# Normalizing the last five tiles of a transform one by one instead of together

## The chip, the cores and the metric

The kernel runs on one core of a Trainium2 chip. The metric is the device time of one execution in microseconds. Engines are called as in the profile: PE is TensorE (PEld its weight loads), DVE is VectorE, ACT is ScalarE, POOL is GpSimd, SP is SyncE.

## The reference, cut to what matters

A graph network of four layers on 1250 nodes with 512 features. The change lies at the end of the first layer, whose second part computes, for 21250 edges,

```python
hb = einsum('nd,bdo->bno', h, basis1)              # four bases
m = (sum over b of comp1[etypes][:, b] * hb[b][src]) * norm
out = segment_sum(m, dst) + bias1 + h @ loop1
x = layernorm(x + out)                             # mean and variance over 512 columns, eps 1e-5
```

The next layer then gathers rows of this `x` by `src`, again for 21250 edges.

## The kernel before, in words

The nodes lie in ten tiles of 128 rows (NT = 10, HALF = 5). A part of a layer has two stages. `aggregate` gathers rows with indirect DMAs that POOL issues (`gather`, L740), multiplies them on PE by a selector (L788), adds them into `G` on DVE (L909) and turns the sums with PE transposes. `transform` then multiplies the turned sums by the bases.

`transform` runs over 32 steps in the part that matters here: two halves of five tiles, and in each half four bases by four blocks of 128 rows. In a step ACT rounds the left side and the weights (L1267, L1269), DVE and POOL make the remainders (L1285, L1297), and PE does three matmuls for each of the five tiles (L136 to L138, in `split_matmul`), tile j into PSUM bank j. Only the fifteenth matmul of a step counts up the semaphore `product` (`multiplied`). Where there is no bias, as here, the epilogue takes "the half is summed" from that semaphore.

The epilogue is `ResidualNorm`. For the first half its work is strewn between the steps of the second (`between_on_dve`, `between_on_act`). For the second half it comes behind the last step, as five instructions of each kind in a row:

- DVE, in `add` (L1202), adds bank j to the residual tile in SBUF, five times, after it has waited for the whole half; then it waits until these are done.
- DVE, in `moments`, does five `bn_stats` (L1004), waits, five `bn_aggr` (L1007), and in `add_eps` one addition of eps to the five variances (L1019).
- ACT, in `root` (L1024), takes the five square roots in one instruction.
- DVE, in `norm`, takes five reciprocals in one instruction (L1029), and subtracts and multiplies each tile in place (L1032, a `tensor_scalar` with the mean and the reciprocal as scalars of a partition), five times.
- ACT, in `store`, waits for each tile and issues its store to `x1_rows` (L1177, 256 KB each, on ACT's own DMA queue).

What comes next in program order is `aggregate` of the second layer. Its first instruction on POOL is a memset of 24 windows of the new `G` (L747, 128 by 12288 fp32 in SBUF), which waits only until the last left side of the transform has been read. Everything else, on PE, ACT, DVE and POOL alike, waits for the list `ready`: the last product, the ten normalized tiles and the landing of all five stores:

```python
ready = multiplied + [residual.ln.normed.now()] + [s.now() for s in residual.stored]
```

POOL then issues the gathers, at first eleven, and each later one when the matmul that frees its buffer is done. DVE builds the selectors (L843, L850), and ACT zeroes the other 57 windows of `G` (L823). The third transform (second layer) has a bias, and its own epilogue lies partly in the third layer.

Of the kernel before, what the change touches and what calls it, by code (L numbers as in the profile page):

```python
# [5 lines left out]
ALU = mybir.AluOpType  # L6
ACT = mybir.ActivationFunctionType
# [16 lines left out]
HALF = NT // 2  # L24
# [105 lines left out]
def tile_rows(r, j):  # L130
    return r[j * P:(j + 1) * P, :]


def split_matmul(pe, acc, lhs, rhs, start, stop):

    pe.matmul(acc, lhs[0], rhs[0], start=start, stop=False)  # L136
    pe.matmul(acc, lhs[0], rhs[1], start=False, stop=False)  # L137
    return pe.matmul(acc, lhs[1], rhs[0], start=False, stop=stop)  # L138


def prepare(C):
# [292 lines left out]
    def on_pe():  # L434
# [4 lines left out]
        for n in range(at_product[PATHC, "windows", 0], len(products)):  # L439
            multiply(n)  # L440

    on_dve()
    on_pe()
    pool.wait_ge(*taken(at_product[PATH0, "src", 0] + 1))
# [10 lines left out]
def sort_edges(C, load_edges):  # L455
# [66 lines left out]
    on_sp()  # L522
    on_pool()
    on_dve()
    cleared = C.event("sort_cleared")
    for engine in (act, pool):
# [13 lines left out]
class Coefficients:  # L540
# [133 lines left out]
    def on_dve(self):  # L674
        for k in range(len(self.batches)):
            self.compare(k)
            if k and self.complete(k - 1) is not None:
                self.weigh(k - 1)
        self.weigh(len(self.batches) - 1)
# [22 lines left out]
def aggregate(C, path, nb, co, rows, G, slots, ready, free=(), cleared=0, counting=None,  # L702
# [216 lines left out]

    on_pool()  # L920
    on_act()
    on_pe()
    on_dve()
    M.at = space
    if counting:
# [110 lines left out]
class TransposeX:  # L1036
# [26 lines left out]
    def on_act(self):  # L1063
        act = self.C.act
        for j in range(0, NT, 2):
            act.wait_ge(*self.turned(j + 1))
            act.copy(*self.moved(j)).then_inc(*self.by_act.inc())
        act.wait_ge(*self.by_dve(NT // 2))
# [72 lines left out]
class ResidualNorm:  # L1141
# [24 lines left out]
        pass  # L1166

    def on_act(self, half):
        self.ln.root(HALF, half + 1)
        self.store(half)  # L1170

# [24 lines left out]
    def add(self, half):  # L1196
# [5 lines left out]
            dve.tensor_tensor(self.tile(j), C.bank[j % HALF][:], self.tile(j), ALU.add).then_inc(*self.added.inc())  # L1202
        dve.wait_ge(*self.added.now())

    def on_dve(self, half):
        tiles = [self.tile(j) for j in range(half * HALF, (half + 1) * HALF)]
        self.add(half)
        self.ln.moments(tiles)
        self.ln.norm(tiles, half + 1)


def transform(C, products, bias, ready, epilogue, extra=None, beside=0, other=None):

    M, bank = C.M, C.bank
    pe, act, dve, pool, sp = C.engines
    ring = M.new("weight_ring", [P, 4, D])
    weight_parts = M.new("weight_parts", [P, 2, 2, D], F32R)
    lhs_parts = M.new("lhs_parts", [P, 2, 2, HALF, P], F32R)  # L1220
    brow = M.new("bias_row", [1, D])
    steps = [(half, m, k) for half in range(2) for m in range(len(products)) for k in range(KC)]
    middle = len(steps) // 2
    chunk_in = [C.landed(f"chunk{r}_in") for r in range(4)]
    bias_in = C.landed("bias_rows_in")
    lhs_hi, lhs_lo = C.event("lhs_hi"), C.event("lhs_lo")
    weight_hi, weight_lo = C.event("weight_hi"), C.event("weight_lo")
    multiplied, summed = C.event("product"), C.event("half_summed")
    epilogue.summed = summed if bias is not None else lambda half: multiplied(half * middle)
    epilogue.half_read = lhs_lo(middle)  # L1230
    if other:
        other.half_read, other.weight_lo = lhs_lo(middle), weight_lo

    def on_sp():
        for token in ready:
            sp.wait_ge(*token)
        if bias is not None:
            sp.dma_start(brow[:], bias.rearrange("(a d) -> a d", a=1)).then_inc(*bias_in.inc())
        for n, (half, m, k) in enumerate(steps):
            if n == middle + 4:  # L1240
                epilogue.on_sp(0)
            if extra and n == extra.at - 6:
                extra.load()
            if extra and 4 <= n < 4 + NT // 2:
                for j in range(2 * (n - 4), 2 * (n - 4) + 2):
                    C.count_store.row(j)
            if other and n >= middle:
                other.on_sp(n - middle)
            if n >= 4:
                sp.wait_ge(*weight_lo(n - 4 + 1))  # L1250
            sp.dma_start(ring[:, n % 4, :], products[m][1][k * P:(k + 1) * P, :]).then_inc(*chunk_in[n % 4].inc())
        epilogue.on_sp(1)

    def on_act():
        for token in ready:
            act.wait_ge(*token)
        for n, (half, m, k) in enumerate(steps):
            if extra and n == extra.at:
                extra.on_act()
            if n > middle:  # L1260
                epilogue.between_on_act(n - middle)
            if other and n >= middle:
                other.on_act(n - middle)
            lhs = products[m][0](k, range(half * HALF, (half + 1) * HALF))
            if n >= 2:
                act.wait_ge(*multiplied(n - 2 + 1))
            act.copy(lhs_parts[:, n % 2, 0], lhs).then_inc(*lhs_hi.inc())  # L1267
            act.wait_ge(*chunk_in[n % 4](n // 4 + 1))
            act.copy(weight_parts[:, n % 2, 0, :], ring[:, n % 4, :]).then_inc(*weight_hi.inc())  # L1269
        if not other:  # L1270
            epilogue.on_act(1)

    def on_dve():
        for token in ready:
            dve.wait_ge(*token)
        for n, (half, m, k) in enumerate(steps):
            if extra and n == extra.at:
                extra.on_dve()
            if n > middle:
                epilogue.between_on_dve(n - middle)  # L1280
            if other and n >= middle:
                other.on_dve(n - middle)
            lhs = products[m][0](k, range(half * HALF, (half + 1) * HALF))
            dve.wait_ge(*lhs_hi(n + 1))
            dve.tensor_tensor(lhs_parts[:, n % 2, 1], lhs, lhs_parts[:, n % 2, 0].bitcast(F32),  # L1285
                              ALU.subtract).then_inc(*lhs_lo.inc())
        if not other:
            epilogue.on_dve(1)

    def on_pool():  # L1290
        for token in ready:
            pool.wait_ge(*token)
        for n in range(len(steps)):
            if other and n >= middle:
                other.on_pool(n - middle)
            pool.wait_ge(*weight_hi(n + 1))
            pool.tensor_tensor(weight_parts[:, n % 2, 1, :], ring[:, n % 4, :],  # L1297
                               weight_parts[:, n % 2, 0, :].bitcast(F32), ALU.subtract).then_inc(*weight_lo.inc())

    def on_pe():  # L1300
        for token in ready:
            pe.wait_ge(*token)
        for n, (half, m, k) in enumerate(steps):
            if extra and n == extra.at - 1:
                extra.on_pe()
            if other and n >= middle:
                other.on_pe(n - middle)
            s = n % 2
            pe.wait_ge(*lhs_lo(n + 1))
            pe.wait_ge(*weight_lo(n + 1))  # L1310
            for j in range(HALF):
                if n == middle:
                    epilogue.wait_for_bank(j)
                ins = split_matmul(pe, bank[j][:], [lhs_parts[:, s, q, j, :] for q in range(2)],
                                   [weight_parts[:, s, q, :] for q in range(2)], m == 0 and k == 0,
                                   bias is None and n % middle == middle - 1)
            ins.then_inc(*multiplied.inc())
            if n % middle == middle - 1:
                if bias is not None:
                    pe.wait_ge(*bias_in(1))  # L1320
                    for j in range(HALF):
                        ins = pe.matmul(bank[j][:], C.ones[0:1, :], brow[:], start=False, stop=True)
                    ins.then_inc(*summed.inc())
                epilogue.on_pe(half)

    on_sp()
    on_act()
    on_dve()
    on_pool()
    on_pe()  # L1330
    return [multiplied.now(), summed.now()], [lhs_lo(len(steps) - beside)]

# [44 lines left out]
def layers_0_1(C):  # L1377
# [19 lines left out]
    hidden = Hidden(C, h, xT, hidden_rows)  # L1397
    turn_x = TransposeX(C, x, xT, 4 * KC)
    multiplied, free = transform(C, products + [(plain_lhs(xT), A["L0_gnn_loop0"])], A["L0_gnn_bias0"], turned, hidden,
                                 turn_x, KC)  # L1400
    assert M.at <= tail
# [176 lines left out]
def layer_2(C):  # L1578
# [145 lines left out]
    on_sp()  # L1724
    on_pe()
    on_act()
    on_dve()
    C.layer2_done = [z_taken.now(), degree.now(), turned_act.now(), turned_dve.now(), C.conditioned]
# [874 lines left out]
```

## Time and profile before

| | |
|---|---|
| median of 3 runs | 3517.71 us (3515.36 to 3524.45) |
| time of the profiled execution | 3515.15 us |
| its span | 3513.8 us |
| PE, DVE, ACT, POOL busy | 91%, 55%, 40%, 34% of the span |
| mean granted PE clock | 0.974 |

The span is the time between the first and the last instruction that the profiler saw; 1.35 us of the execution's time lies around it. The profile's busy shares are averages over stages with different limits, so one stage has to be read from the timeline and the chain of waits.

### The profile page before, as it was taken

Reading aid. Unit: us, or ns where it says so; the run is one execution under the profiler, and the core shown is the slowest. Engines: PE = TensorE matmul, PEld = TensorE weight load, DVE = VectorE, ACT = ScalarE, POOL = GpSimd, SP = SyncE. Lnnn points to the kernel's source line nnn. Section 1 sums busy time; section 2 is a strip of 40 time slices with the busy share of each in tenths; the row PEclk is TensorE's granted clock in tenths of the full one; section 3 lists DMA queues with packets and bytes.
Section 4 is the critical chain, followed back from the end, with each engine's and each line's share of the span. In section 5 each row is a group of like instructions: output and inputs, shape, how many; then the busy total and the mean of one; then the engine's idle time right before and its main releaser. Section 6 shows DMA issues by size and latency. Waiting matters only on the chain.

```text
span 3513.8 us, 38688 instructions
## 1 busy us (share of the span) xinstructions
PE 3186.8 (91%) x13432; PEld 2126.0 (61%) x13432; DVE 1926.9 (55%) x4296; ACT 1417.8 (40%) x2263; POOL 1186.4 (34%) x1003
## 2 busy tenths in 40 slices
PE   5999898999977788999988999999999999989998
PEld 2333576444742246775456777777777776777767
DVE  6999522887357763245363446544365444754356
ACT  6888632001340023342244553245432554435444
POOL 3666335776367763342000012300132001410022
PEclk8999998999999999999999999999999999999999
DMA  3555433766247763333011001300113001120012
GB/s 85 160 162 161 157 115 103 203 198 183 77 135 211 210 191 103 87 95 114 12 51 42 7 31 44 114 13 7 60 39 95 7 7 61 49 86 7 7 60 72
DMA packets 137266, 318.07 MB, mean 91 GB/s; under 512 B 25380, under 2 KB 43108, under 8 KB 136046
## 3 DMA queue, kind: packets, MB, share of 16 engines
q0 software_dynamic: 53040, 173.84, 17.4%
q1 hardware_dynamic: 82590, 139.10, 12.6%
q8 instruction: 110, 1.80, 0.2%
q10 hardware_dynamic: 1440, 2.62, 0.2%
q14 instruction: 86, 0.70, 0.1%
HBM read 269.50 MB, written 24.84 MB: 84 GB/s over the span
## 4 chain that ended last, share of the span: by engine, by line
PE 71%; DVE 14%; ACT 6%; issue 6%; DVEq 2%; DMA 1%; POOL 1%; SPq 1%; POOLq 0%; ACTq 0%
PE bank L136 11%; PE bank L138 11%; PE bank L137 11%; PE bank L788 10%; PE bank L2282 10%; PE bank L2267 5%; DVE G L909 4%; PE bank L798 3%; PE bank L1983 2%; PE bank L1632 2%; ACT prob L2354 2%; ACT probT L2330 1%; PE bank L766 1%; DVE x_stats L1918 1%; DVE y_tile L1935 1%
## 5 line engine op out<-in xcount | busy, mean ns | idle before, releaser
L788 PE MATMUL bank<-gathered,selector 128*128 128x512 f32 x1326 | 669.1, 619 | 130.6 <-DVE G L909 88.9
L909 DVE TENSOR_TENSOR G<-G,bank 128x512 f32 x663 | 453.7, 684 | 168.6 <-PE bank L788 96.2
L788 PEld LDWEIGHTS bank<-gathered,selector 128*128 128x128 f32 x1326 | 217.2, 194 | 424.4 <-issue 361.2
L2399 DVE CUSTOM_DVE_ANT_0 prob<-bank,count_by_src 128x512 f32<-128x512 f32 (+1 forms) x480 | 258.5, 589 | 316.2 <-PE bank L138 316.2
L2282 PE MATMUL bank<-probT,values_and_heads 128*128 128x512 f32 (+1 forms) x960 | 366.7, 522 | 6.0 <-DVE values_and_heads L2380 6.0
L1297 POOL TENSOR_TENSOR weight_parts<-weight_ring,weight_parts 128x512 fp32r<-128x512 f32 x136 | 199.9, 1471 | 391.5 <-ACT weight_parts L1269 391.5
L2330 ACT COPY probT<-bank 128x512 f32<-128x512 f32 (+1 forms) x480 | 199.0, 488 | 291.7 <-PE bank L2267 291.7
L814 ACT ACTIVATE sign_src<-node_iota_16bit,src_float 128x1280 bf16<-128x1280 f16 x208 | 282.2, 1361 | 50.9 <-PE bank L798 45.0
L775 ACT COPY G<-bank 128x512 f32<-128x512 f32 x160 | 81.3, 659 | 546.2 <-PE bank L766 546.2
L136 PE MATMUL bank<-weight_parts,lhs_parts 128*128 128x512 f32 x680 | 271.7, 400 | 29.4 <-POOL weight_parts L1297 26.6
L1285 DVE TENSOR_TENSOR lhs_parts<-G,lhs_parts 128x640 fp32r<-128x640 f32 x128 | 107.2, 838 | 336.4 <-ACT lhs_parts L1267 336.2
L740 POOL DMA_INDIRECT gathered<-in_x,src_index x208 | 219.2, 1054 | 162.4 <-PE bank L788 100.0
L137 PE MATMUL bank<-weight_parts,lhs_parts 128*128 128x512 f32 x680 | 269.7, 397 | 0.0
L138 PE MATMUL bank<-weight_parts,lhs_parts 128*128 128x512 f32 x680 | 269.0, 396 | 0.0
L740 POOL DMA_INDIRECT gathered<-x_rows,src_index x247 | 233.5, 945 | 92.0 <-issue 50.9
L2111 POOL TENSOR_TENSOR lhs_parts<-values_and_heads,lhs_parts 128x512 fp32r<-128x512 f32 x80 | 107.4, 1347 | 418.0 <-ACT lhs_parts L2091 417.6
L2354 ACT ACTIVATE prob<-prob,negated_max 128x1250 f32<-128x1250 f32 x160 | 218.9, 1368 | 70.3 <-DVE negated_max L2406 70.3
L1836 POOL CAST head_weights_hi<-head_weights 128x1024 fp32r<-128x1024 f32 x16 | 16.6, 1036 | 675.8 <-DMA head_bias_cols<-in_L_gnn_bk 675.8
L2282 PEld LDWEIGHTS bank<-probT,values_and_heads 128*128 128x128 f32 x960 | 172.2, 191 | 114.8 <-issue 108.1
L2267 PE MATMUL bank<-ident,prob 128*128 128x128 f32 x1600 | 204.9, 275 | 30.1 <-ACT prob L2354 29.7
L136 PE MATMUL bank<-kT_hi,qT_hi 128*128 128x512 f32 (+1 forms) x480 | 203.7, 424 | 21.7 <-DVE span_max L2399 17.0
L740 POOL DMA_INDIRECT gathered<-hidden_rows,src_index x208 | 197.5, 950 | 75.9 <-issue 43.6
(272 smaller groups left out, 6225.8 us busy)
## 6 DMA issues: line engine op xcount, KB each, us to landing
weight_ring<-in_L_gnn_basis SPq DMA_DIRECT2D x64, 256.0 KB, 2.7
weight_ring<-in_L_gnn_bases SPq DMA_DIRECT2D x64, 256.0 KB, 2.6
x_L<-x_rows SPq DMA_DIRECT2D x50, 256.0 KB, 4.4
x_rows<-x_L SPq DMA_DIRECT2D x40, 256.0 KB, 2.0
yT_hi<-yT_new_hi SPq DMA_DIRECT2D x4, 2560.0 KB, 10.9
yT_lo<-yT_new_lo SPq DMA_DIRECT2D x4, 2560.0 KB, 10.9
count_rows<-count SPq DMA_DIRECT2D x10, 640.0 KB, 5.6
count_by_dst<-count_rows SPq DMA_DIRECT2D x10, 640.0 KB, 9.4
```

Source lines behind the costliest of these rows:

```text
L136: pe.matmul(acc, lhs[0], rhs[0], start=start, stop=False)
L137: pe.matmul(acc, lhs[0], rhs[1], start=False, stop=False)
L138: return pe.matmul(acc, lhs[1], rhs[0], start=False, stop=stop)
L740: pool.indirect_dma_start(xs[:, s % slots, :], None, rows, bass.IndirectOffsetOnAxis(ap=C.src_i[path][:, s:s + 1], axis=0)).then_inc(*gath ...
L788: pe.matmul(bank[s % banks][:], sel[:, s % SELECTORS, :], xs[:, s % slots, :], start=True, stop=True).then_inc(*multiplied.inc())
L814: act.activation(counting.sign_src[:, q, :], counting.iota16[:], ACT.Sign, bias=C.src_f[:, s:s + 1], scale=-1.0).then_inc(*signed.inc())
L909: dve.tensor_tensor(g, g, bank[s % banks][:], ALU.add).then_inc(*added.inc())
L2267: ins = pe.transpose(bank[3 + q // 4][0:width, (q % 4) * P:(q % 4 + 1) * P], prob[:, t % 2, q * P:q * P + width], C.ident[:])
L2282: ins = pe.matmul(bank[6][:, 0:many * P], slots[0:width, 1 + h, q * P:(q + 1) * P], PT[0:width, G % 2, q, 0:many * P], start=q == 0, stop= ...
L2330: act.copy(PT[:, G % 2, 4 * b:4 * b + many, cols], bank[3 + b][:, 0:many * P].rearrange("p (q n) -> p q n", n=P))
L2354: act.activation(prob[:, t % 2, :], prob[:, t % 2, :], ACT.Exp, bias=nmax[:, t % 2:t % 2 + 1], scale=scale, accum_out=rsum[:, h % 2, t:t + ...
L2399: dve.tensor_tensor_reduce(out=prob[:, s, c:c + width], in0=bank[n][:, 0:width], in1=count[:, t, c:c + width], scale=1.0, scalar=-2.0 * NE ...
```

## The change

Where the transform has no bias, `transform` hands its epilogue a list `tile_summed`: one semaphore value for each of the five tiles of the last step. For this the third matmul of tiles 0 to 3 of the last step now counts up the semaphore `half_summed`, and tile 4 has the last product as before. When the list is there, `ResidualNorm` does its second half in `last_on_dve` and `last_on_act`. DVE goes tile by tile: wait for the bank, add, wait, `bn_stats`, wait, `bn_aggr`; and behind the statistics of tile j it normalizes tile j - 1 (`last_norm`: a reciprocal of one column, a wait, the `tensor_scalar`). ACT takes one square root for each tile, with eps as the bias of the activation, so that `add_eps` goes; and between the roots it issues the stores, tile by tile. The first half, and transforms with a bias, stay as they were.

```diff
     def on_act(self, half):
+        if half and self.tile_summed:
+            return self.last_on_act()
         self.ln.root(HALF, half + 1)
         self.store(half)
...
+    def last_on_dve(self):
+
+        C, dve, ln = self.C, self.C.dve, self.ln
+        for j in range(HALF):
+            tile = self.tile(HALF + j)
+            dve.wait_ge(*self.tile_summed[j])
+            dve.tensor_tensor(tile, C.bank[j][:], tile, ALU.add).then_inc(*self.added.inc())
+            dve.wait_ge(*self.added.now())
+            dve.bn_stats(C.stat[:, j, :], tile).then_inc(*ln.chain.inc())
+            dve.wait_ge(*ln.chain.now())
+            dve.bn_aggr(C.mv[:, j, :], C.stat[:, j, :]).then_inc(*ln.measured.inc())
+            if j:
+                self.last_norm(j - 1)
+        self.last_norm(HALF - 1)
+
+    def last_norm(self, j):
+        C, dve, ln = self.C, self.C.dve, self.ln
+        tile = self.tile(HALF + j)
+        dve.wait_ge(*ln.rooted(j + 2))
+        dve.reciprocal(C.rstd[:, j, :], C.rstd[:, j, :]).then_inc(*ln.chain.inc())
+        dve.wait_ge(*ln.chain.now())
+        dve.tensor_scalar(tile, tile, C.mv[:, j, 0:1], C.rstd[:, j, :], ALU.subtract, ALU.mult).then_inc(*ln.normed.inc())
+
+    def last_on_act(self):
+        C, act, ln = self.C, self.C.act, self.ln
+        for j in range(HALF + 1):
+            if j < HALF:
+                act.wait_ge(*ln.measured(j + 2))
+                act.activation(C.rstd[:, j, :], C.mv[:, j, 1:2], ACT.Sqrt, bias=C.eps[:]).then_inc(*ln.rooted.inc())
+            if j:
+                n = HALF + j - 1
+                act.wait_ge(*ln.normed(n + 1))
+                act.dma_start(tile_rows(self.rows, n), self.tile(n)).then_inc(*self.stored[j - 1].inc())
+
     def on_dve(self, half):
+        if half and self.tile_summed:
+            return self.last_on_dve()
...
     epilogue.summed = summed if bias is not None else lambda half: multiplied(half * middle)
+    epilogue.tile_summed = None if bias is not None else [
+        summed(j + 1) if j < HALF - 1 else multiplied(len(steps)) for j in range(HALF)]
...
                                    bias is None and n % middle == middle - 1)
+                if bias is None and n == len(steps) - 1 and j < HALF - 1:
+                    ins.then_inc(*summed.inc())
             ins.then_inc(*multiplied.inc())
```

## Rows read from the trace of the kernel before

**Rows 1.** The page's part 4, shares of the chain that ended last, by engine

```profile
PE 71%; DVE 14%; ACT 6%; issue 6%; DVEq 2%; DMA 1%; POOL 1%; SPq 1%; POOLq 0%; ACTq 0%
```

**Rows 2.** The chain of waits from 985 to 1045 us: start, length, what

```profile
1012.87 2.88 DMA x_rows<-x
```

**Rows 3.** Timeline of TensorE, last step: start, length, instruction, idle before and its releaser

```profile
999.44 0.39 PE L136 MATMUL bank<-weight_parts,lhs_parts 128*128 128x512 f32 x1
...
999.90 0.39 PE L138 MATMUL bank<-weight_parts,lhs_parts 128*128 128x512 f32 x1
...
1002.62 0.39 PE L138 MATMUL bank<-weight_parts,lhs_parts 128*128 128x512 f32 x1
```

**Rows 4.** Timeline of VectorE after the last step

```profile
1003.04 3.08 DVE L1202 TENSOR_TENSOR x<-bank,x 128x512 f32<-128x512 f32 x5 [5.21 <-PE bank L138]
...
1006.16 3.07 DVE L1004 BATCH_NORM_STATS2 ln_stats<-x 128x6 f32<-128x512 f32 x5
...
1009.74 0.17 DVE L1019 TENSOR_SCALAR ln_rstd<-ln_mean_var 128x5 f32<-128x5 f32 x1
...
1010.19 0.19 DVE L1029 RECIPROCAL ln_rstd<-ln_rstd 128x5 f32<-128x5 f32 x1 [0.27 <-ACT ln_rstd L1024]
...
1010.41 2.37 DVE L1032 TENSOR_SCALAR x<-x,ln_mean_var,ln_rstd 128x512 f32<-128x512 f32 x5
```

**Rows 5.** Timeline of ScalarE and GpSimd over the same stretch

```profile
1010.99 2.39 ACTq L1177 DMA_DIRECT2D x_rows<-x  x5
...
998.93 10.35 POOL L747 MEMSET G<- 128x12288 f32 x1
...
1016.51 0.97 POOL L740 DMA_INDIRECT gathered<-x_rows,src_index  x1 [7.24 <-DMA x_rows<-x]
...
1017.78 0.95 POOL L740 DMA_INDIRECT gathered<-x_rows,src_index  x1 [0.30 <-issue]
```

**Rows 6.** Single instructions of L1202, 998 to 1013 us: ns min/median/max

```profile
L1202 DVE TENSOR_TENSOR x<-bank,x x5: 681/682/692, 1003.0 to 1005.4; 128x512 f32<-128x512 f32 x5
```

**Rows 7.** Timeline of VectorE, one aggregate of the first half

```profile
951.69 0.18 DVE L1014 BATCH_NORM_AGGREGATE ln_mean_var<-ln_stats 128x2 f32<-128x6 f32 x1
```

**Rows 8.** Timelines of VectorE and GpSimd where two instructions meet

```profile
970.39 1.30 DVE L1032 TENSOR_SCALAR x<-x,ln_mean_var,ln_rstd 128x512 f32<-128x512 f32 x1
...
970.00 1.41 POOL L1297 TENSOR_TENSOR weight_parts<-weight_ring,weight_parts 128x512 fp32r<-128x512 f32 x1 [1.99 <-ACT weight_parts L1269]
...
1502.57 0.81 DVE L1552 TENSOR_SCALAR turn<-angle 64x1280 f32<-64x1280 f32 x1
...
1504.80 1.92 DVE L1555 TENSOR_SCALAR turn<-turn 64x1280 f32<-64x1280 f32 x1
...
1504.62 1.41 POOL L1297 TENSOR_TENSOR weight_parts<-weight_ring,weight_parts 128x512 fp32r<-128x512 f32 x1 [1.99 <-ACT weight_parts L1269]
```

**Rows 9.** Timelines of GpSimd and VectorE during a shorter memset

```profile
2161.34 0.95 POOL L1845 MEMSET modulation_loaded<- 96x1024 f32 x1
...
2162.25 0.16 DVE L1926 SCALAR_TENSOR_TENSOR x_shift<-x_mean_var,x_rstd 128x1 f32<-128x1 f32 x1
```

**Rows 10.** L1024 in the whole run: ns min/median/max, first and last start

```profile
L1024 ACT ACTIVATE ln_rstd<-ln_rstd x4: 204/208/211, 967.8 to 1620.0; 128x5 f32<-128x5 f32 x4
...
L1024 ACT ACT_TABLE_LOAD  x2: 1283/1283/1283, 966.5 to 1618.7; - x2
```

**Rows 11.** The stores of L1177 from 1009 to 1017 us: issue to landing

```profile
DMA to landing us min/median/max: 2.0/2.5/2.9
```

**Rows 12.** Windows: length, each engine's busy us, granted clock, DMA share, GB/s

```profile
1024.00:1026.00 2.00, 2.00 (x5) 0.76 (x4) 1.23 (x2) 2.00 (x1) 1.68 (x2) 0.78 0.72 221
```

**Rows 13.** Timelines of TensorE and VectorE, start of the next gather loop

```profile
1020.05 7.36 PE L788 MATMUL bank<-gathered,selector 128*128 128x512 f32 x11 [17.05 <-DMA gathered<-x_rows,src_index]
...
1022.24 0.69 DVE L909 TENSOR_TENSOR G<-G,bank 128x512 f32 x1 [2.08 <-PE bank L788]
...
1025.41 0.69 DVE L909 TENSOR_TENSOR G<-G,bank 128x512 f32 x1 [0.77 <-PE bank L788]
```

## The prediction

> **What bounds the kernel now.** I read the page first: PE makes 71% of the chain that ended last [rows 1], so PE sets most of the time. But the change touches only the seam between the second transform and the next gather loop, and there the average says nothing. So I took the chain of waits and the timelines around 1000 us. PE's last matmul of the transform starts at 1002.62 [rows 3]. Then only the epilogue runs: DVE adds from 1003.04, takes statistics from 1006.16, the reciprocals at 1010.19, and normalizes from 1010.41 for 2.37 us, to 1012.78 [rows 4]. ACT issues five stores from 1010.99 on [rows 5]. The chain goes through the last of them, which begins at 1012.87 and takes 2.88 us, to 1015.75, and 0.76 us later, at 1016.51, POOL's first gather begins [rows 2, 5]. PE, DVE and ACT wait for the same landing. This seam is on the path in full, with nothing beside it that is needed; a microsecond by which the last store lands earlier or later moves all that follows by a microsecond. One thing does lie beside it: POOL's memset of the new G, from 998.93 to 1009.28 [rows 5]. It is hidden now, and the reader should keep it in mind.
>
> **The earlier start.** The last step's first matmul starts at 999.44, tile 0's third at 999.90, tile 4's third at 1002.62 [rows 3], so tiles are finished 0.68 us apart. Today DVE starts 0.42 us after that third matmul of tile 4 began. By the same lag tile 0 can be added at 999.90 + 0.42 = 1000.32, 2.72 us earlier than now. The four new counts on PE's matmuls I cost at nothing: they ride on instructions that are there, and fifteen matmuls of a step are still in the same order. PE has in any case nothing after them.
>
> **The longer DVE work.** One add takes 0.68 us [rows 6], but five in a row take 3.08 [rows 4], that is 0.60 each: with no wait between, the next starts about 0.08 before the end. With a wait the gap is 0.04 the other way (the adds end at 1006.12, the statistics begin at 1006.16). So for one tile, counted from the start of its add: add 0.68 and gap 0.04; statistics about the same, 0.68 and 0.04; aggregate 0.18 [rows 7]; the next independent instruction begins 0.08 before that ends, at 1.54. A reciprocal to its tensor_scalar is 0.22 (1010.19 to 1010.41), and five tensor_scalars in 2.37 us are 0.46 apart and 0.54 long [rows 4]. A tile with the normalization of the one before thus takes 1.54 + 0.22 + 0.46 = 2.22 us, and the first tile 1.54 alone. Gone is the addition of eps, 0.17 us [rows 4].
>
> ACT's five roots instead of one are 0.21 us each [rows 10]. They lie beside DVE's work: root j is due only after the statistics of tile j + 1, or, for the last, behind the normalization of tile 3 (0.68 us, against 0.21 and two hand-overs). A table load would be 1.28 us. The run has one in this transform, at 966.5, and the root at the end has none of its own [rows 10]; only casts and stores lie between, and the new roots have only stores between them. So none; the upper bound is one that isn't covered, 1.28 us.
>
> If nothing else happened: tile 0's add at 1000.32, tile 1's at 1001.86, tile 0's tensor_scalar at 1003.62, tile 2's add at 1004.08, tile 3's at 1006.30, tile 4's at 1008.52, the normalization of tile 3 at 1010.06, of tile 4 at 1010.74, its tensor_scalar at 1010.96, end 1011.50. Against 1012.78 that is 1.28 us gained.
>
> **What the tensor_scalars now meet.** Today they run from 1010.41, after the memset has ended at 1009.28. After the change the first would start at 1003.62, in the middle of it. Rows show what happens when this kind of instruction starts while POOL works. At 970.39 one took 1.30 us instead of 0.54; POOL's instruction ran from 970.00 to 971.41, and the tensor_scalar ended at 971.69, 0.28 after it. At 1504.80 one of L1555 took 1.92 us where its like, L1552, took 0.81; POOL ended at 1506.03, it ended at 1506.72 [rows 8]. Both stood still until POOL's instruction was over, and then did the work. Adds from a bank and statistics don't: they kept 0.68 and 0.60 us under the memset [rows 4 to 6]. Those two POOL instructions read and wrote SBUF, and a memset only writes. Under a shorter memset from 2161.34 to 2162.29 a DVE instruction with two operands in SBUF took 0.16 us [rows 9], unhindered; no row has a tensor_scalar of a tile under a memset. So the bound from below is no wait, the bound from above a wait to the memset's end, 1009.28 - 1003.62 = 5.66 us. I take the wait, because the two rows of the very same kind of instruction are nearer than one of another kind.
>
> The Trainium skill, "SBUF — State Buffer", section "Who interferes with whom", says that a VectorE instruction in a two-port mode, which a tensor_scalar may take, and any GpSimd instruction lock each other out for the whole instruction, while two SBUF inputs only collide with a GpSimd instruction that reads. By it the memset blocks too, and the sum is the higher one; it speaks against this change. The rows agree for instructions that read and write; for a memset none here shows it.
>
> With the wait: the first tensor_scalar ends at 1009.28 + 0.28 = 1009.56. DVE runs in order, so the adds of tiles 2 to 4, whose banks are long ready, are queued behind it, and with them ACT's roots and stores and all of `ready`. Tile 2's add comes at 1009.48, tile 3's at 1011.70, tile 4's at 1013.92, the reciprocal of tile 3 at 1015.46, of tile 4 at 1016.14, the last tensor_scalar from 1016.36 to 1016.90. Against 1012.78 that is 4.12 us lost.
>
> **The stores.** The last store now takes 2.88 us from its issue [rows 2] because five follow closely; the range is 2.0 to 2.9 [rows 11]. After the change they are 2.2 us apart but for the last two, 0.7 apart, so I take 2.2, nearer the lone one. The last lands at 1016.90 + 0.09 + 2.2 = 1019.19 against 1015.75: +3.4 us (with 2.88 it is +4.1). ACT's issues are 2.39 us for five [rows 5] and fit between the tiles.
>
> **Behind the seam** everything waits on the same landing, so it moves as one: POOL's gathers at 1.27 us each, which set the pace at first (1016.51 to 1017.78, [rows 5]), ACT's zeroing, the selectors. Nothing gives time back, for nothing else was late. The sum is 3515.15 + 3.4 = 3518.6 for the profiled execution. The median shown is 2.56 above that execution, so as a median I expect 3517.71 + 3.4 = 3521.1. That is 0.1%, less than the 0.3% (10.6 us) that a measurement of this kernel can tell from no change.
>
> **The rivals.**
>
> - The memset doesn't hold the tensor_scalar up. For it: the 0.16 us under a memset [rows 9]. Against it: rows 8. Then DVE gains 1.3 and the last store about 0.6: 3517.71 - 1.9 = 3515.8.
> - PE's clock returns later, and the kernel is slower. PE's idle stretch grows by 3.4 us, from 17.05 to some 20.5 [rows 13]. Now the granted clock is back within 1024 to 1026 (mean 0.78, [rows 12]), and until then the accumulations at 1022.24 and 1025.41 are two steps, so 1.59 us for one, against 1.27 that POOL needs [rows 13, 5]. Each further step at 1.2 GHz costs 0.32 us. It decides only from (10.6 - 3.4)/0.32, about 23 further steps; with 27, 3517.71 + 3.4 + 8.6 = 3529.7. Against it: the clock rose soon after work came back, after an idle time nearly as long.
> - The change doesn't do what it says, and tile 0's count is seen only with the last. The add starts at 1003.04, the first tensor_scalar at 1006.34, and if the memset blocks, it ends at 1009.56 all the same: the time of my forecast. If the memset doesn't block, DVE ends at 1014.22, 1.4 us later than now, and with a store of 2.2 the time is 3518.5.
>
> **How the numbers follow.** My forecast has 0.70, the free memset 0.22, the late clock 0.05, the unheard counts without blocking 0.03. The first, second and fourth lie within 0.3%. From the first I take 0.03 for a median that lands above that bound by scatter (the three runs shown span 9 us), and 0.02 from the second for one below. So: faster 0.02, same 0.90, slower 0.08. The range reaches from the free memset less the 2.35 us that the lowest run lies under the median, 3513.5, to the store's upper end, 3521.8, plus some 4 of scatter, 3526. That leaves out the late clock and the tails.
>
> **What would show it.** Right: L1202's single instructions of this seam start at 1000.3 and 1001.9, then a gap to about 1009.5; the first new tensor_scalar (`last_norm`) lasts some 5.9 us and ends 0.3 after the memset; the other four last 0.54; the tiles come 2.2 apart; the last normalization ends near 1016.9, the first gather begins near 1020. Five roots of 0.21 and no further table load. Wrong: a first tensor_scalar of 0.54 us, with the first gather near 1014.6; a memset longer than 10.35 us, which would mean that DVE takes turns with it; adds that begin at 1003; a granted clock of 0.50 after 1030.

## The result, and the profile after

The changed kernel takes 3526.47 us (median of 20 runs, 3519.79 to 3534.50); the kernel before, measured beside it, 3519.20 us (20 runs, 3514.20 to 3529.32). The ratio is 1.0017 with a 95% interval of 1.0010 to 1.0024: 6 us more, within 0.3%. The forecast was 3.4 us more, 0.1%.

The whole span is a poor place to see a few microseconds: the 20 executions of the kernel before lie 15 us apart, and 35 of them in a later measurement 22 us. The seam shows a few microseconds clearly: it came out within 0.02 us whenever a kernel was profiled again. I call **seam** the time from the start of the last matmul of the second transform to the start of the first gather of the next loop. Before, it is 1016.51 - 1002.62 = 13.89 us [rows 3, 5].

TensorE in the profile after, last step and the first matmuls of the next loop (start, length, instruction, idle before and its releaser):

```profile
1008.12 0.39 PE L138 MATMUL bank<-weight_parts,lhs_parts 128*128 128x512 f32 x1
...
1028.61 2.05 PE L788 MATMUL bank<-gathered,selector 128*128 128x512 f32 x2 [20.10 <-DMA gathered<-x_rows,src_index]
```

ScalarE and GpSimd, timelines of the same stretch:

```profile
1007.50 0.29 ACT L1235 ACTIVATE ln_rstd<-ln_mean_var,eps 128x1 f32<-128x1 f32 x1 [4.50 <-DVE ln_mean_var L1217]
...
1004.43 10.35 POOL L747 MEMSET G<- 128x12288 f32 x1
...
1025.07 0.97 POOL L740 DMA_INDIRECT gathered<-x_rows,src_index  x1 [10.28 <-DMA x_rows<-x]
```

The first gather starts at 1025.07, so the seam is 1025.07 - 1008.12 = 16.95 us, 3.06 more than before. The memset starts 3.69 us before the last matmul, exactly as before (1002.62 - 998.93), and is as long. The five roots are now single ones, and there is no table load.

VectorE, the lines that answer to [rows 4]:

```profile
1005.83 0.69 DVE L1213 TENSOR_TENSOR x<-bank,x 128x512 f32<-128x512 f32 x1 [2.49 <-PE bank L138]
...
1006.56 0.69 DVE L1215 BATCH_NORM_STATS2 ln_stats<-x 128x6 f32<-128x512 f32 x1
...
1007.28 0.18 DVE L1217 BATCH_NORM_AGGREGATE ln_mean_var<-ln_stats 128x2 f32<-128x6 f32 x1
...
1009.07 5.99 DVE L1228 TENSOR_SCALAR x<-x,ln_mean_var,ln_rstd 128x512 f32<-128x512 f32 x1
...
1014.98 0.67 DVE L1213 TENSOR_TENSOR x<-bank,x 128x512 f32<-128x512 f32 x1
...
1016.68 0.55 DVE L1228 TENSOR_SCALAR x<-x,ln_mean_var,ln_rstd 128x512 f32<-128x512 f32 x1
...
1018.86 0.55 DVE L1228 TENSOR_SCALAR x<-x,ln_mean_var,ln_rstd 128x512 f32<-128x512 f32 x1
...
1021.68 0.55 DVE L1228 TENSOR_SCALAR x<-x,ln_mean_var,ln_rstd 128x512 f32<-128x512 f32 x1
```

Read them in order. The first add begins at 1005.83, 2.29 us before the last matmul does; before, it began 0.42 us after. So the early release works. Add, statistics and aggregate follow each other with gaps of 0.03 to 0.04. Then the first normalization (L1228) takes 5.99 us where the others take 0.55. It ends at 1015.06, and GpSimd's memset has ended at 1004.43 + 10.35 = 1014.78, 0.28 us before. Only then comes the third tile's add, at 1014.98, though its bank had been ready since about 1007. From there a tile comes every 2.17 us, and the last normalization ends at 1022.23, 14.11 us after the last matmul began, against 10.16 before.

The chain that ended last now goes through that one instruction (start, length, what; the rows between the first and the last normalization are left out):

```profile
1009.07 5.99 DVE x L1228
...
1021.68 0.56 DVE x L1228
...
1022.26 2.04 DMA x_rows<-x
```

The last store takes 2.04 us instead of 2.88 [rows 2]. The stores are now spread, and all five land equally soon, as the landing times of L1239 show, against [rows 11]. In `norms_last` below, where five stores follow closely again, the last takes 2.90 us.

```profile
DMA to landing us min/median/max: 2.0/2.0/2.1
```

### The profile page after: what moved, and what is told of

The parts are those of the page before. It is cut to its first block, busy times and chain, and to the rows that moved or that the text cites. A ratio compares the mean times of both kernels' runs of the same rounds, so it can differ in the third digit from the quotient of the medians.

```text
span 3529.8 us, 38674 instructions
## 1 busy us (share of the span) xinstructions
PE 3193.7 (90%) x13411; PEld 2130.1 (60%) x13432; DVE 1934.5 (55%) x4299; ACT 1419.2 (40%) x2267; POOL 1188.3 (34%) x1003
## 4 chain that ended last, share of the span: by engine, by line
PE 70%; DVE 15%; issue 6%; ACT 6%; DVEq 2%; DMA 1%; POOL 1%; SPq 1%; POOLq 0%; ACTq 0%
PE bank L136 11%; PE bank L138 11%; PE bank L137 11%; PE bank L788 10%; PE bank L2324 9%; PE bank L2309 5%; DVE G L909 4%; PE bank L798 3%; PE bank L2025 2%; PE bank L1674 2%; ACT prob L2396 2%; ACT probT L2372 1%; DVE x_stats L1960 1%; DVE y_tile L1977 1%; PE bank L766 1%
## 5 line engine op out<-in xcount | busy, mean ns | idle before, releaser
L1337 POOL TENSOR_TENSOR weight_parts<-weight_ring,weight_parts 128x512 fp32r<-128x512 f32 x136 | 201.1, 1480 | 397.5 <-ACT weight_parts L1309 397.5
L1325 DVE TENSOR_TENSOR lhs_parts<-G,lhs_parts 128x640 fp32r<-128x640 f32 x128 | 107.1, 837 | 343.2 <-ACT lhs_parts L1307 343.0
```

## The experiments

All traces are compared by their seam. The lock theory of the expectations says that the memset holds the first normalization up until it is over. The batch with `pieces_with_gaps`, `norms_last_again` and `norms_last_short`, and `after_third`, ran where both kernels take some 100 us more (median of the kernel before 3621 and 3622 us), nearly all of it in the two gather loops before and behind this seam; of these runs I use ratios and seams alone. The two kernels that ran here and in another batch as well have the same seams in both, to 0.02 us.

| run | first normalization, us | last one ends after the last matmul's start, us | seam, us | ratio to before (95%) |
|---|---|---|---|---|
| before, `before_again` | 0.55, no cover | 10.16 | 13.89 | 0.9997 (0.9984 to 1.0010) |
| after | 5.99 | 14.11 | 16.95 | 1.0017 (1.0010 to 1.0024) |
| `after_again` | 6.00 | 14.10 | 16.93 | 1.0009 (0.9997 to 1.0022) |
| `late_counts` | 3.27 | 14.10 | 16.93 | 1.0012 (0.9998 to 1.0026) |
| `memset_behind` | 0.55 | 8.66 | 19.29 | 1.0017 (1.0006 to 1.0029) |
| `memset_pieces` | 6.92 | 15.03 | 17.87 | 1.0010 (0.9997 to 1.0024) |
| `pieces_with_gaps` | 1.18 | 11.00 | 13.84 | one run, no ratio |
| `other_form` | 0.75 | 9.69 | 12.51 | 0.9997 (0.9984 to 1.0011) |
| `norms_last` | 0.93 | 8.75 | 12.50 | 0.9998 (0.9986 to 1.0009), as `norms_last_again` |
| `norms_last_pieces` | 1.84 | 9.66 | 13.39 | 0.9994 (0.9982 to 1.0005) |
| `norms_last_short` | 0.55 | 8.38 | 12.12 | 0.9999 (0.9986 to 1.0011) |
| `after_third` | 6.00 | 14.11 | 16.94 | 1.0003 (0.9985 to 1.0020) |

### before_again, after_again, after_third: the two kernels, unchanged

> The kernel before, unchanged, for scatter. I call seam the time from the start of the last matmul of the second transform to the start of the first gather of the next loop: 13.9 us in the trace before, 17.0 in the trace after. Both theories (the memset holds the first tensor_scalar up and that is all; or the change also costs something outside the seam) expect ratio 1.000 within 0.1% and a seam of 13.9 here. What it tells: how much the stages outside the seam differ from one execution of the same kernel to the next. If the stage from the first gather of the second layer to the first memset of the third layer's modulation tile (595.3 us before, 602.8 after) comes out up to 7 us longer here too, that part of the difference is scatter.

> The changed kernel, unchanged. Seam 17.0 us. If only the seam costs, the ratio tends to 1.001 and the stage behind the seam lies as often near 595 as near 603 us; if the change costs something behind the seam as well, that stage is near 603 us again and the ratio near 1.002.

> The changed kernel once more, timed, to see whether more than the seam costs. Seam 17.0 us again. If the seam is all, 3.1 us of 3520, the ratio is 1.0009; if there is more behind it, 1.0017 as in the first measurement. One interval is about 0.12% either way, so this can only shift the balance.

The seams came out as 13.89, 16.93 and 16.94 us, so the 3.06 us are no scatter. The stage behind the seam, 595.3 us before and 602.8 after, was 599.3 us in `before_again` and 597.5 in `after_again`: it varies by some 4 us in the kernel before as well. The two further ratios of the changed kernel, 1.0009 and 1.0003, lie lower than the first.

### late_counts: all five tiles released by the last product

```diff
-        summed(j + 1) if j < HALF - 1 else multiplied(len(steps)) for j in range(HALF)]
+        multiplied(len(steps)) for j in range(HALF)]
```

> The changed kernel with all five tiles released by the last product, as before the change; all else as changed. Lock theory: the first add starts 0.4 us after the last matmul begins, the first tensor_scalar 3.7 us after it, and still ends with the memset, so it lasts 3.0 us instead of 6.0 and the seam stays 17.0 us. Rival (the interleaved order itself is slow, not the memset): the seam grows by the 2.7 us that the work starts later, to 19.7.

VectorE's timeline, and the memset:

```profile
1003.83 0.69 DVE L1213 TENSOR_TENSOR x<-bank,x 128x512 f32<-128x512 f32 x1 [5.21 <-PE bank L138]
...
1007.07 3.27 DVE L1228 TENSOR_SCALAR x<-x,ln_mean_var,ln_rstd 128x512 f32<-128x512 f32 x1
```

```profile
999.72 10.35 POOL L747 MEMSET G<- 128x12288 f32 x1
```

Counted from the last matmul's start, the first add begins 2.7 us later than in the changed kernel. The normalization begins later too, at 1007.07, lasts 3.27 us instead of 5.99, and ends at 1010.34, 0.27 us after the memset (999.72 + 10.35 = 1010.07). From there all is the same, and the seam is 16.93. By the rival, that the interleaved order itself is slow, it would have been 19.7. What the change won by starting early was all lost in one wait, whose end neither start moves.

### memset_behind: the memset after the normalized tiles

```diff
+            if cleared < path.windows + 1:
+                for token in ready[:3]:
+                    pool.wait_ge(*token)
             pool.memset(G[:, 0:cleared, :], 0.0).then_inc(*zeroed_pool.inc())
```

> The changed kernel with POOL's memset moved behind the ten normalized tiles, so that it meets no tensor_scalar; it is then on the path. Lock theory: the first tensor_scalar lasts 0.54 us, the last ends 8.9 us after the last matmul began, the memset follows and ends near 19.3, and the seam is 19.4 us. Rival (the tensor_scalar waits for something else, such as its root or the bank): it still lasts some 6 us, the normalization ends 14.3 us after the last matmul began, and the seam is near 25.

VectorE's first normalization, and GpSimd:

```profile
1008.97 0.55 DVE L1231 TENSOR_SCALAR x<-x,ln_mean_var,ln_rstd 128x512 f32<-128x512 f32 x1
...
1016.83 10.34 POOL L750 MEMSET G<- 128x12288 f32 x1 [12.44 <-DVE x L1231]
...
1027.32 0.97 POOL L740 DMA_INDIRECT gathered<-x_rows,src_index  x1 [0.15 <-issue]
```

With nothing on GpSimd the first normalization takes 0.55 us, and the last ends 8.66 us after the last matmul's start (8.88 worked out before). So the 5.99 us of the changed kernel were no wait for a root or a bank. The memset now stands on the path, which is why this kernel has the longest seam.

### memset_pieces and pieces_with_gaps: when is the lock given up?

```diff
-            pool.memset(G[:, 0:cleared, :], 0.0).then_inc(*zeroed_pool.inc())
+            if cleared < path.windows + 1:
+                for w in range(cleared - 1):
+                    pool.memset(G[:, w:w + 1, :], 0.0)
+                pool.memset(G[:, cleared - 1:cleared, :], 0.0).then_inc(*zeroed_pool.inc())
+            else:
+                pool.memset(G[:, 0:cleared, :], 0.0).then_inc(*zeroed_pool.inc())
```

`cleared` is the number of windows that GpSimd clears; the condition leaves a memset of the whole `G`, as in other places, in one piece.

> The changed kernel with the memset cut into 24 of one window (512 columns) each. If the lock is held for one instruction and given up between two: the first tensor_scalar (0.9 us after the last matmul begins) waits for at most one piece, some 0.5 us, so it lasts 0.6 to 1.1 us, the others up to 1.1; the last ends 9 to 11.5 us after the last matmul began instead of 14.1, and the seam is 12 to 14.3 us instead of 17.0. Rival: POOL takes the next piece before VectorE gets in, and the first tensor_scalar waits for all of them, until about 9 us: seam 19. The memset itself takes some 12.5 us in sum instead of 10.35, or more where it waits for VectorE.

```profile
1008.24 6.92 DVE L1233 TENSOR_SCALAR x<-x,ln_mean_var,ln_rstd 128x512 f32<-128x512 f32 x1
...
1003.61 10.81 POOL L749 MEMSET G<- 128x512 f32 x23
...
1014.34 0.54 POOL L750 MEMSET G<- 128x512 f32 x1
```

The rival held, and my first expectation missed. There are 24 instructions, none of which takes more than 0.54 us. The first normalization began at 1008.24 and ended at 1015.16, 0.28 us after the last of them (1014.34 + 0.54 = 1014.88). VectorE's tensor_scalar never came in between two. The Trainium skill, "SBUF — State Buffer", section "Who interferes with whom", speaks of a lock held for the whole instruction; by this run it is in effect held over a row of instructions that follow each other without a gap.

```diff
-            pool.memset(G[:, 0:cleared, :], 0.0).then_inc(*zeroed_pool.inc())
+            if cleared < path.windows + 1:
+                part_cleared = C.event("part_cleared")
+                for w in range(0, cleared - 4, 4):
+                    pool.memset(G[:, w:w + 4, :], 0.0).then_inc(*part_cleared.inc())
+                    pool.wait_ge(*part_cleared.now())
+                pool.memset(G[:, cleared - 4:cleared, :], 0.0).then_inc(*zeroed_pool.inc())
...
```

> The changed kernel with the memset in six pieces of four windows (some 1.8 us each), and POOL waits for the end of each before it starts the next. In the run with 24 pieces one behind the other VectorE did not get in between. If that was because POOL's next piece was already queued when the former ended, a gap lets VectorE in: the first tensor_scalar lasts at most 1.8 + 0.5 us, the last ends 9 to 12 us after the last matmul began, seam near 12 to 15, and one POOL piece is lengthened. Rival (VectorE gets the lock only when POOL has nothing left): the first tensor_scalar lasts 6 to 7.5 us again, seam 17 to 18.5.

The first three normalizations, and the third to sixth memset:

```profile
1039.58 1.18 DVE L1235 TENSOR_SCALAR x<-x,ln_mean_var,ln_rstd 128x512 f32<-128x512 f32 x1
...
1042.38 0.55 DVE L1235 TENSOR_SCALAR x<-x,ln_mean_var,ln_rstd 128x512 f32<-128x512 f32 x1
...
1044.55 2.26 DVE L1235 TENSOR_SCALAR x<-x,ln_mean_var,ln_rstd 128x512 f32<-128x512 f32 x1
...
1038.67 1.80 POOL L750 MEMSET G<- 128x2048 f32 x1
...
1040.53 1.96 POOL L750 MEMSET G<- 128x2048 f32 x1
...
1042.55 2.11 POOL L750 MEMSET G<- 128x2048 f32 x1
...
1044.72 1.80 POOL L752 MEMSET G<- 128x2048 f32 x1
```

Now GpSimd waits for each piece before it starts the next. The first normalization, from 1039.58, ends at 1040.76, 0.29 us after the third piece (1038.67 + 1.80). It came in before the fourth, which starts at 1040.53 and is lengthened to 1.96 us. The second begins at 1042.38, 0.11 us before the end of the fourth piece (1042.49), gets in, takes its usual 0.55 us, and the fifth piece is lengthened to 2.11. The third begins at 1044.55, again 0.11 us before the end of a piece (1044.66), but does not get in: it lasts 2.26 us, until 0.29 us after the sixth piece (1044.72 + 1.80). So a gap of 0.06 us let VectorE in twice and failed it once. What decides between the second case and the third no run shows. The seam is 13.84, that of the kernel before: the harm is gone, and so is the gain.

### other_form: the same values by a slower form of instruction

```diff
-        dve.tensor_scalar(tile, tile, C.mv[:, j, 0:1], C.rstd[:, j, :], ALU.subtract, ALU.mult).then_inc(*ln.normed.inc())
+        dve.scalar_tensor_tensor(tile, tile, C.mv[:, j, 0:1], C.rstd[:, j, :].to_broadcast([P, D]), ALU.subtract,
+                                 ALU.mult).then_inc(*ln.normed.inc())
```

> The changed kernel with a scalar_tensor_tensor in place of the tensor_scalar: the same values, but the reciprocal comes as a second SBUF operand repeated over the columns, so that the instruction makes one column a cycle (some 0.69 us, 0.61 apart) and not two. If what the memset locks out is the form that does two columns a cycle: no wait, each lasts 0.69 us, the last ends about 9.6 us after the last matmul began, seam 12.4 us. Rival (a memset locks out every VectorE instruction that writes SBUF from SBUF operands, or a second SBUF operand collides with it): the first lasts some 6 us and the seam is 17.5 us or more.

First and last normalization, and GpSimd:

```profile
1005.13 0.75 DVE L1228 SCALAR_TENSOR_TENSOR x<-x,ln_mean_var,ln_rstd 128x512 f32<-128x512 f32 x1
...
1013.13 0.75 DVE L1228 SCALAR_TENSOR_TENSOR x<-x,ln_mean_var,ln_rstd 128x512 f32<-128x512 f32 x1
...
1000.50 10.35 POOL L747 MEMSET G<- 128x12288 f32 x1
...
1016.70 0.97 POOL L740 DMA_INDIRECT gathered<-x_rows,src_index  x1 [5.85 <-DMA x_rows<-x]
```

The first normalization runs from 1005.13 to 1005.88 in the middle of a memset that lasts from 1000.50 to 1010.85, and isn't held up. The memset isn't held up either, 10.35 us. So the memset doesn't bar VectorE from SBUF; it holds the tensor_scalar up and lets the scalar_tensor_tensor pass. The edit changes the kind of instruction and its speed together. Two places in the trace of the kernel before say more. The first has a tensor_scalar that reads a bank in PSUM instead of SBUF. It runs at the slower pace (0.68 us for 512 columns, against 0.55 from SBUF) and isn't held up: this one, of 256 columns, took its usual 0.42 us and ended 0.27 us before the GpSimd instruction around it:

```profile
1666.73 0.42 DVE L1718 TENSOR_SCALAR count_by_src<-bank 128x256 f32<-128x256 f32 x1 [0.53 <-PE bank L1642]
...
1666.15 1.27 POOL L1838 TENSOR_TENSOR input_weights_lo<-input_weights,input_weights_hi 128x512 fp32r<-128x512 f32 x1
```

So it isn't the kind of instruction alone that is held up, but, as far as these rows go, the fast pass from SBUF to SBUF. The second place is a limit of the remedy. It has a scalar_tensor_tensor, as in this run with two operands in SBUF, beside a GpSimd instruction that reads SBUF, which a memset doesn't. It took 1.40 us instead of its usual 0.16 (the median of its 90 instances) and ended at 2171.14, 0.02 us after GpSimd's (2168.73 + 2.39 = 2171.12):

```profile
2169.74 1.40 DVE L1926 SCALAR_TENSOR_TENSOR x_shift<-x_mean_var,x_rstd 128x1 f32<-128x1 f32 x1
...
2168.73 2.39 POOL L1864 TENSOR_TENSOR modulation_parts<-modulation_loaded,modulation_parts 32x1024 fp32r<-32x1024 f32 x1
```

The slower form passes under a memset, then, and not under every GpSimd instruction. Here, 0.75 us against 0.55, it gives a seam 4.4 us shorter than the changed kernel's and 1.4 shorter than the kernel before's. This is near what the change would have given by the rival of a free memset (1.9 us).

### norms_last, norms_last_pieces, norms_last_short: normalize at the end

```diff
             dve.bn_aggr(C.mv[:, j, :], C.stat[:, j, :]).then_inc(*ln.measured.inc())
-            if j:
-                self.last_norm(j - 1)
-        self.last_norm(HALF - 1)
+        dve.wait_ge(*ln.rooted(HALF + 1))
+        dve.reciprocal(C.rstd[:], C.rstd[:]).then_inc(*ln.chain.inc())
+        dve.wait_ge(*ln.chain.now())
+        for j in range(HALF):
+            dve.tensor_scalar(self.tile(HALF + j), self.tile(HALF + j), C.mv[:, j, 0:1], C.rstd[:, j, :],
+                              ALU.subtract, ALU.mult).then_inc(*ln.normed.inc())
```

ScalarE takes the five roots and then issues the five stores (that part of the edit is left out above). `norms_last_pieces` adds the 24 memsets of `memset_pieces`; `norms_last_short` lets GpSimd clear 20 windows and ScalarE the other 61:

```diff
-                       (after_G - C.after_layer1_edges) // (4 * D) // 2)
+                       (after_G - C.after_layer1_edges) // (4 * D) // 2 - 4)
```

> The changed kernel with the order on VectorE turned: adds and statistics of all five tiles as they come, the normalizations behind them, as one reciprocal and five tensor_scalars; the stores behind the roots. Lock theory: statistics end 5.4 us after the last matmul began, the first tensor_scalar starts near 5.7 and ends with the memset at 6.9 (1.3 us long), the last ends at 8.8 instead of 14.1, the stores are close together again and the last takes 2.9 us: seam 12.5 us, 1.4 below the kernel before. Rival (the early release is itself no gain): seam 13.9 or more.

> norms_last once more, timed. Seam 12.5 us as before. Ratio to the kernel before 0.9996 if only the seam counts, an interval of 0.1% either way; against the changed kernel some 4.5 us less.

> As norms_last, and the memset in 24 pieces. If the lock is given up between pieces: first tensor_scalar waits at most 0.5 us, the last ends 8.0 to 9.5 us after the last matmul began, seam 11.7 to 13.2 us. If POOL keeps it: the first waits until about 9 us, seam 14.6.

> norms_last, and POOL clears 20 windows of G instead of 24 (ScalarE clears 61 instead of 57, some 26.2 us instead of 24.5, needed by VectorE's step 20, still some 7 us later). The memset is 8.6 us and ends 5.0 us after the last matmul began, before the first tensor_scalar at 6.0: all five in 2.37 us, the last ends at 8.4 instead of 8.8, seam 12.1 us. If seam 12.5, something other than the memset held the first one of norms_last.

The five normalizations and GpSimd in `norms_last`:

```profile
1007.53 2.74 DVE L1222 TENSOR_SCALAR x<-x,ln_mean_var,ln_rstd 128x512 f32<-128x512 f32 x5
...
997.83 10.35 POOL L747 MEMSET G<- 128x12288 f32 x1
...
1014.02 0.97 POOL L740 DMA_INDIRECT gathered<-x_rows,src_index  x1 [5.84 <-DMA x_rows<-x]
```

The same in `norms_last_short`:

```profile
1046.22 2.37 DVE L1222 TENSOR_SCALAR x<-x,ln_mean_var,ln_rstd 128x512 f32<-128x512 f32 x5
...
1036.52 8.64 POOL L747 MEMSET G<- 128x10240 f32 x1
...
1052.33 0.97 POOL L740 DMA_INDIRECT gathered<-x_rows,src_index  x1 [7.16 <-DMA x_rows<-x]
```

In `norms_last` adds and statistics, which the memset doesn't hold up, fill the time until the memset is nearly over. The five normalizations take 2.74 us instead of 2.37, because the first begins 0.65 us before the memset ends (997.83 + 10.35 = 1008.18) and lasts 0.93 us. With a memset of 8.64 us, which ends 4.95 us after the last matmul's start, they take 2.37 us again, and the seam is 12.12 us, 1.77 below the kernel before. `norms_last_pieces` failed for the same reason as `memset_pieces`: a longer memset, seam 13.39. Expected was 11.7 to 13.2, or 14.6 by the rival; it lies between, since the pieces were done sooner (7.6 us after the last matmul's start) than the 9 that I had put. In the whole time none of these gains can be shown; for `norms_last_short` the ratio is 0.9999 with an interval of 0.13% either way, and 1.77 us are 0.05%.

## Why the prediction was right

That the total came out within 0.3% says little for the mechanism: by the forecast and by two of its three rivals alike it had to. The seam has to bear the argument. The trace after runs 5.50 us later than the trace before (last matmul at 1008.12 and 1002.62), so 5.50 has to be added to the times of day that the prediction names.

- **The seam is on the path in full.** Right. The chain goes through the epilogue, the last store and the first gather in both kernels.
- **The earlier start.** Expected 2.72 us earlier; measured 0.42 + 2.29 = 2.71.
- **The longer DVE work.** Expected 2.22 us for a tile; measured 2.17 (1016.68 to 1018.86). The roots take 0.29 us each and not 0.21, without a table load, all hidden.
- **The tensor_scalar meets the memset.** This was the step that chose the sign, between no wait and 5.66 us. Expected 5.9 us long and an end 0.28 after the memset; measured 5.99 and 0.28. That an instruction held up does its columns only after GpSimd's has ended fits two lengths: 512 columns end 0.28 us after GpSimd's instruction, and the 1280 columns of L1555 0.69 us after [rows 8], which is 0.55 and 0.54 ns for a column. `memset_behind` shows the memset as the cause, by taking it away, and `other_form`, with the row of L1718 beside it, that it is a matter of the instruction's form. The row of another kind of instruction under a memset [rows 9] was no evidence against it. It overlapped the memset only in the memset's last 0.04 us (2162.25 to 2162.29), and in `pieces_with_gaps` even a tensor_scalar that began 0.11 us before a memset's end took its usual 0.55. Besides, it was a scalar_tensor_tensor, like `other_form`, and that isn't held up by a memset. So the row, which the prediction read as unhindered and as its rival's evidence, could not tell the two apart.
- **The rest is queued behind it.** Expected an end 14.28 us after the last matmul's start; measured 14.11.
- **The stores.** Expected 2.2 us for the last, measured 2.04; together with the tile spacing this makes the seam's growth 3.06 and not 3.4 us.
- **Nothing gives time back.** Right within the scatter. The clock came back as before. After the first matmul of the loop at 1028.61, the granted clock was 0.50 (1.2 GHz) until 1032, 0.54 from 1032 to 1034 and 1.00 (2.4 GHz) from there; before, after a first matmul at 1020.05, it was 0.50 until 1024, 0.78 from 1024 to 1026 and 1.00 from there. (The sign "a granted clock of 0.50 after 1030" has to be moved by the same 5.50 us; taken as written it would have come true for a reason that has nothing to do with the rival.) The first three accumulations were 1.71 and 1.65 us apart, 3.36 us in sum against 3.17 [rows 13], and the fourth came 0.90 behind the third. The rival of a late clock fell; its price here is 0.2 us.

VectorE's first accumulations of the next loop after the change:

```profile
1030.80 0.69 DVE L909 TENSOR_TENSOR G<-G,bank 128x512 f32 x1 [2.10 <-PE bank L788]
...
1032.51 0.69 DVE L909 TENSOR_TENSOR G<-G,bank 128x512 f32 x1 [1.02 <-PE bank L788]
...
1034.16 0.69 DVE L909 TENSOR_TENSOR G<-G,bank 128x512 f32 x1 [0.96 <-PE bank L788]
...
1035.06 0.69 DVE L909 TENSOR_TENSOR G<-G,bank 128x512 f32 x1 [0.21 <-PE bank L788]
```

- **The rival of the unheard counts** had the same time as the forecast under a blocking memset; `late_counts` confirms that to 0.02 us. The counts themselves are heard: the first add begins before the last matmul.

The total agrees less well than the seam. The median, 3526.47 us, is 5.4 above the forecast of 3521.1 and 0.5 above the end of its range, 3526. Part of that is the base: the kernel before took 3519.20 us in the comparison, not the 3517.71 of its first three runs, and 3517.71 times 1.0017 is 3523.7, within the range. The growth is 6 us by the ratio where 3.4 were forecast. 3.06 us are 0.09%, and the first ratio has its lower end at 1.0010, just above that share. With the two further comparisons the weighted mean (each by the inverse square of its interval's width) is 1.0014, with some 0.0006 either way. The seam alone is within that, near its lower end. Whether the changed kernel costs another microsecond or two elsewhere isn't settled. No trace shows a place for it, and the longer stage behind the seam occurs in both kernels. So the mechanism of the 3.06 us is shown, and for the rest the forecast lies near by a margin that nothing here explains.

## What to carry to other kernels

Before an instruction is moved to an earlier time, look at what runs then on the other engines; a free slot on its own engine is not enough. Here a memset on GpSimd stretched one VectorE instruction from 0.55 to 5.99 us. Where an instruction can wait long in order, everything behind it in the queue waits too, so put first what can't be held up (here the adds and statistics) and last what can. When the gain is below the scatter of the whole, measure it between two events in the trace that lie close to the change.

## What the runs showed of the hardware that was not expected

Twenty-four memsets in a row held VectorE's tensor_scalar off just as one long one did, and gave a longer wait (6.92 us against 5.99). A gap of 0.06 us between two GpSimd instructions let a waiting tensor_scalar in at two places and not at a third.

In the third transform, which the change doesn't touch, it is GpSimd that is held up. In the kernel before, its instruction L1297 takes 4.19 us instead of 1.41, while long reciprocals run on VectorE:

```profile
1536.08 4.19 POOL L1297 TENSOR_TENSOR weight_parts<-weight_ring,weight_parts 128x512 fp32r<-128x512 f32 x1 [1.67 <-ACT weight_parts L1269]
...
1535.12 3.34 DVE L1565 RECIPROCAL cond_sigmoid<-cond_sigmoid 16x512 f32<-16x512 f32 x1
...
1539.07 3.33 DVE L1565 RECIPROCAL cond_sigmoid<-cond_sigmoid 16x512 f32<-16x512 f32 x1
```

In the profile after, the same instruction (now L1337) takes 8.11 us, under the same sequence on VectorE:

```profile
1548.52 3.33 DVE L1607 RECIPROCAL cond_sigmoid<-cond_sigmoid 16x512 f32<-16x512 f32 x1
...
1551.77 0.75 DVE L1325 TENSOR_TENSOR lhs_parts<-G,lhs_parts 128x640 fp32r<-128x640 f32 x1
...
1545.53 8.11 POOL L1337 TENSOR_TENSOR weight_parts<-weight_ring,weight_parts 128x512 fp32r<-128x512 f32 x1 [1.68 <-ACT weight_parts L1309]
```

In the first it got in where one reciprocal follows another (it ended at 1540.27, 1.20 us after the second had begun at 1539.07); in the second it missed that place and ended at 1553.64, 1.19 us after the third had begun at 1552.45. What holds it isn't settled. The second reciprocal takes 3.33 us in both traces, though GpSimd's instruction finishes beside it in the one and not in the other, and between two reciprocals VectorE runs an instruction that reads two operands in SBUF (L1325 above). Which of the two happens is not a property of the change: the longest instance of this line was 8.11 us in `before_again` (the kernel before) and in `other_form`, and 4.19 in `after_again`. Of the ten traces of the faster batches, the three with 8.11 have 599.3, 602.8 and 603.5 us for the stage behind the seam; the seven others have 595.3 to 597.5. That it is this missed place that makes the stage longer was not tested by a run of its own. But it is a hint of where some of the scatter of this kernel comes from.
